# One signal per two steps: TensorE raises `summed` on every second sum, VectorE adds two banks per signal

## The reference

```python
def gnn(h, edge_index, W, b):               # h = layernorm(x)
    src, dst = edge_index
    msg_sum = segment_sum(h[src], dst, n)   # 100000 rows gathered and summed by destination
    deg = segment_sum(ones, dst, n)
    agg = msg_sum / maximum(deg, 1.0)[:, None]
    return concatenate([h, agg], axis=1) @ W.T + b

def ffn(x):                                 # x = layernorm of the first layer's result
    xn = layernorm(x) * gamma + beta
    logits = xn @ Wr + br
    w, idx = softmax of the top 2 of 8 logits
    for e in range(8):
        y += (gelu(xn @ W1[e] + b1[e]) @ W2[e] + b2[e]) * w_of(e)
    return y

x = x + gnn(layernorm(x)); x = x + ffn(layernorm(x))
```

## Time and profile before

| what | us |
|---|---|
| median of 3 runs | 1471.27 (1469.2 to 1472.08) |
| the profiled execution's own time | 1469.85 |
| its span, first to last instruction | 1468.5 |
| TensorE busy | 1154.8 (79%) |
| GpSimd busy | 1076.8 (73%) |
| VectorE busy | 766.6 (52%) |
| ScalarE busy | 501.5 (34%) |
| mean granted clock of TensorE | 0.904 |

### The profile page before, as it was taken

The page is one execution under the profiler, slowest core; times in us unless marked ns, Lnnn a source line. Parts: engine busy times, 40 slices in busy tenths (PEclk is TensorE's granted clock), DMA queues, the critical chain, the costliest instruction groups (busy, mean ns, idle before and its releaser), DMA issues.

```text
span 1468.5 us, 22976 instructions
## 1 busy us (share of the span) xinstructions
PE 1154.8 (79%) x5570; PEld 881.0 (60%) x5570; DVE 766.6 (52%) x2642; ACT 501.5 (34%) x1088; POOL 1076.8 (73%) x1032
## 2 busy tenths in 40 slices
PE   3277898779767987697979768888897978878895
PEld 2234535547535776376768547656776766656795
DVE  7666645645553555346446534644646465554321
ACT  3500004103202442144335215324353444345574
POOL 2477777677777777777777777777777777773677
PEclk9999998889877999789999869989998988988998
DMA  9943665344444554445455454545454454453444
GB/s 333 300 138 105 227 199 168 115 129 124 120 127 129 135 122 123 120 124 135 123 134 120 120 129 123 130 116 137 123 131 122 120 130 125 120 126 92 70 70 44
DMA packets 125080, 197.46 MB, mean 134 GB/s; under 512 B 23954, under 2 KB 94023, under 8 KB 124711
## 3 DMA queue, kind: packets, MB, share of 16 engines
q0 software_dynamic: 63088, 130.30, 36.4%
q1 hardware_dynamic: 59417, 64.89, 14.0%
q10 hardware_dynamic: 2446, 0.80, 0.2%
HBM read 153.82 MB, written 49.27 MB: 138 GB/s over the span
## 4 chain that ended last, share of the span: by engine, by line
PE 49%; issue 13%; POOL 13%; DVE 12%; DMA 7%; ACT 4%; DVEq 2%; ACTq 0%; POOLq 0%; SPq 0%
PE psum L736 17%; PE psum L805 11%; PE psum L830 9%; POOL work L629 7%; DMA work<-h_rows,srcs 4%; PE psum L749 4%; DVE acc L1082 3%; POOL queue L638 3%; POOL out_dram L649 2%; PE psum L750 2%; POOL out_dram L657 1%; PE psum L784 1%; ACT region L534 1%; PE psum L817 1%; PE psum L761 1%
## 5 line engine op out<-in xcount | busy, mean ns | idle before, releaser
L629 POOL DMA_INDIRECT work<-h_rows,srcs x719 | 687.9, 957 | 220.4 <-issue 178.6
L1082 DVE TENSOR_TENSOR acc<-acc,psum 128x257 f32 x830 | 349.5, 421 | 509.7 <-PE psum L736 458.4
L736 PE MATMUL psum<-work 128*128 128x257 f32 x1438 | 468.3, 443 | 140.5 <-DMA work<-h_rows,srcs 70.8
L736 PEld LDWEIGHTS psum<-work 128*128 128x128 f32 x1438 | 270.8, 212 | 256.7 <-DMA work<-h_rows,srcs 123.1
L805 PEld LDWEIGHTS psum<-expert_buf 128*128 128x128 f32 x1680 | 227.2, 212 | 12.6 <-ACT expert_buf L589 5.2
L805 PE MATMUL psum<-expert_buf 128*128 128x128 f32 x1680 | 231.1, 297 | 3.0 <-ACT expert_buf L591 1.4
L830 PE MATMUL psum<-region,expert_buf 128*128 x840 | 202.1, 384 | 3.0 <-ACT expert_buf L591 3.0
L597 ACT ACTIVATE expert_buf<-psum,b_col 128x128 f32<-128x128 f32 x420 | 120.1, 370 | 204.4 <-PE psum L805 201.7
L830 PEld LDWEIGHTS psum<-region,expert_buf 128*128 128x128 f32 x840 | 154.8, 194 | 22.0 <-issue 4.6
L971 DVE TENSOR_TENSOR work<-psum,rel 128x1152 f32<-128x1152 f32 x98 | 126.3, 1289 | 50.6 <-PE psum L736 32.1
L649 POOL DMA_INDIRECT out_dram<-expert_buf,tok_idx x75 | 121.8, 1623 | 22.9 <-issue 20.7
(11 more groups left out here) (245 smaller groups left out, 914.6 us busy)
## 6 DMA issues: line engine op xcount, KB each, us to landing
expert_buf<-queue SPq DMA_DIRECT2D x105, 130.0 KB, 2.7
work<-h_rows,srcs POOLq DMA_INDIRECT x719, 2.8
region<-in_L_ffn_W_dram SPq DMA_DIRECT2D x16, 512.0 KB, 6.4
h_rows<-region SPq DMA_DIRECT2D x7, 896.0 KB, 9.0
own<-h_rows SPq DMA_DIRECT2D x49, 128.0 KB
own<-x_rows SPq DMA_DIRECT2D x49, 128.0 KB
out_dram<-acc SPq DMA_DIRECT2D x49, 128.0 KB, 2.8
region<-in_x_dram SPq DMA_DIRECT2D x6, 896.0 KB, 11.8
```

Of the source, the lines that this page charges most:

```text
L629: pool.indirect_dma_start(place_of(g)[:, 0:D], None, h_rows, bass.IndirectOffsetOnAxis(srcs[:, cell_of:cell_of + 1], 0)).then_inc(got[g % ...
L736: summed.up(pe.matmul(STEP_BANKS[t % BANKS][:, 0:GW], hot[:, k, :], rows, start=True, stop=True))
L1082: added.up(dve.tensor_tensor(sums, sums, STEP_BANKS[t % BANKS][:, 0:GW], ALU.add))
```

## The change

Steps are taken in pairs (2m, 2m+1). Only the matmul of the odd step raises `summed`, and every wait for a step's matmul becomes a wait for its pair:

```diff
     BANKS = 3
+    TOGETHER = 2
+    assert STEPS % TOGETHER == 0
...
+    def signal_of(t):
+
+        return t // TOGETHER
...
 (sync_stream, w1 and w2)
-                    summed.wait(sp, BOTH - 1)
+                    summed.wait(sp, signal_of(BOTH - 1))
-                    summed.wait(sp, BOTH + EXTRA - 1)
+                    summed.wait(sp, signal_of(BOTH + EXTRA - 1))
...
 (gpsimd_stream)
                 if g >= SHARED + EXTRA + RING:
-                    summed.wait(pool, t - RING)
+                    summed.wait(pool, signal_of(t - RING))
...
 (tensor_stream)
                 added.wait(pe, t - BANKS)
-                summed.up(pe.matmul(STEP_BANKS[t % BANKS][:, 0:GW], hot[:, k, :], rows, start=True, stop=True))
+                i = pe.matmul(STEP_BANKS[t % BANKS][:, 0:GW], hot[:, k, :], rows, start=True, stop=True)
+                if t % TOGETHER == TOGETHER - 1:
+                    summed.up(i)
...
 (vector_stream)
                 if k == 0:
...
-                    summed.wait(dve, t - 1)
+                    summed.wait(dve, signal_of(t - 1))
                     one_hot(HALF, SPR - HALF, t + HALF)
...
-                summed.wait(dve, t)
+                summed.wait(dve, signal_of(t))
                 added.wait(dve, t - 1)
                 added.up(dve.tensor_tensor(sums, sums, STEP_BANKS[t % BANKS][:, 0:GW], ALU.add))
```

## The result

| kernel | median | runs |
|---|---|---|
| before | 1470.33 us | 4 (1469.2 to 1472.08) |
| changed | 1520.51 us | 4 (1518.01 to 1521.96) |

The ratio is 1.0342, with a 95% interval of 1.0322 to 1.0361: 50 us slower. The forecast was 1490, its range 1475 to 1508. The direction was right, the size was not, and the time is outside the range. The profiled execution took 1519.08 us (span 1517.8), 49.2 us more than the one of before.

A forecast was written before the change was run, and what follows sets the result against it. GpSimd's gathers were taken to bound 303 to 1167 us, TensorE's sums and VectorE's adds 69 to 282 us. Terms 9 + 4 + 2 + 5 + 0 = +20 us on 1469.85 us gave 1490, range 1475 to 1508.

The forecast's parts named there:

- The loop of two steps over three banks: Add, bank freed, next sum: with pairs two steps to close, 1.41 us a pair in place of 1.27.
- The first 112 steps: Pair loop 5 us, start 0.8, three odd register boundaries 3.8; taken as 9 us, bounds 4 and 12.
- Steps 112 to 219: 36 steps at 0.07 us, routing choice 0.85, some loss at long TensorE items: 4 us, between 0 and 8.
- Time lost on TensorE or VectorE in this stretch is taken out of that slack: 303 to 1167 us, GpSimd the bound: 50 to 80 us of TensorE's time against 193 us slack; 2 us taken.
- Some 85 steps: 1167 to 1331 us, 14 expert tiles, no slack toward gathers: 5 us, bounds 0 and 11.6.
- The middle: 303 to 1167 us: no GpSimd wait over 0.3 us, TensorE's gather waits down to 110 to 140; 2 us.
- Signals: TensorE raises 415 counts less: saving 0 by the trace, 11 us as an estimate from the skill page.
- The tail: After the last step, 138 us without steps: unchanged, 0 us.
- A: Loss stays in the first stretch, gathers absorb the rest: +9 to +12 us, 1479 to 1482; chance 0.22.
- B: Middle tips over, GpSimd stopped again and again: 1528 with half of 80 us unhidden, 1504 with a fifth; chance 0.13.
- C: Hidden anyway, VectorE the slower even with pairs: within 3 us, 1468 to 1474; chance 0.08.
- D: Faster by the clock, half-clock time going in 160 to 282 us and at the end: 1461; chance 0.07.

The follow-up runs named there:

- late adds: Kernel before with all signals kept, but VectorE's add of step t waits for the sum of t|1: 1.0312 and, on another chip, 1.0276.
- the two runs that divide the late adds: Kernel before, even steps' adds late only at 143 steps with other VectorE items behind the add (1.0112), or only at the other 272 (1.0172).
- coarser ring wait: Kernel before, but GpSimd waits for the sum of (t-17)|1 before gather t, where it waited for t-17: 1.001.
- bias-first: Kernel before with four banks, one-hot build from SBUF, single signals, and VectorE's bias add ahead of the step's add: 1515.11 us, 1.0287.

## Why the prediction had the direction right and the size wrong

The terms beside what the lateness table gives:

| term | forecast (bounds) | measured |
|---|---|---|
| steps 0 to 111 | +9 (4 to 12) | +12.1 |
| steps 112 to 219 | +4 (0 to 8) | +9.6 |
| 303 to 1167 us, up to step 638 | +2 (0 to 12), with the next | +1.1 |
| 303 to 1167 us, steps 639 to 745 | in the line above | +11.8 |
| steps 746 to 829 | +5 (0 to 11.6) | +10.7 |
| tail | 0 | +3.9 |
| sum | +20 | +49.2 |

*The loop of two steps over three banks* is right, and shown for the first stretch. 1.41 us a pair was forecast and read. Two banks with single signals, which have the same loop and no late add, take 82.4 us for steps 24 to 111, late adds 80.8, and with a fourth bank the pairs take 74.4, where four banks with single signals take 71.7.

*The first 112 steps* reached the top of the bound. Row by row, the three boundaries cost 1.13, 1.12 and 1.08 us (3.8 forecast for the three), the start 0.45 (0.8), and all the rest 8.3, where I had taken 5. The gather at the ring's end showed it at once, with 12.95 us.

*Steps 112 to 219* were put too low. I priced 36 steps at 0.07 us. With late adds only where neither step of a pair has an item (34 of the 54 pairs) the stretch is 4.8 us longer, about what was forecast for all; with the other 20 pairs it is 9.6. So the other half comes with pairs that have VectorE items, 12 of them right behind the late add, and I had counted one such item, the routing choice. That half is read from one profile each, and the one without it had a granted clock of 0.90 there against 0.87, so part of it can be the clock.

*The step that failed* is "Time lost on TensorE or VectorE in this stretch is taken out of that slack", with the slack read as 193 us, together with "Some 85 steps" without slack behind it. The 193 us counted each wait twice. The matmuls stood 70.4 us for gathers, and the loss that was to go into them was put at 50 to 80. Nor does slack lie in a sum from which losses are paid wherever they fall. A loss is hidden only if the sums catch up with the gathers once more after it. The last catch-up of before is at 1167 us, step 745, but all except 5.9 of the 70.4 us lie ahead of 988 us, step 639. I took the last catch-up from before's trace as fixed. With the loss it moved back to step 639 (1009 us), and the stretch in which each loss counts grew from 85 steps to 190. Its added part, steps 639 to 745, brought 11.8 us. That 36.3 us of the matmuls' waits were left, all ahead of it, shows that their sum was no measure. The move is read from the two traces; no run on a chip like this one had late adds in these steps alone. With only 20 of their 95 pairs late the sums still catch up there, last at 1181 us.

Of the 29.2 us that the forecast fell short by in the profiled execution, 10.9 are in this term (12.9 against 2, over its bound of 12), 5.7 in steps 746 to 829, 5.6 in steps 112 to 219, 3.9 in the tail and 3.1 in the first 112 steps.

*The price of a step without slack* was 0.07 us, and 0.4 us for an expert tile, of which I took less than half; 10.7 us came in steps 746 to 829, just inside the bound I had not believed. Over the 190 steps it is 22.8 us, 0.12 a step. What makes it is open. Late adds from step 640 on cost 15 us (10 to 20) by themselves on the other chips, and TensorE's waits for adds rise from 24.3 to 69.8 us. The loop of two steps is not the whole of it. Over the whole program two banks cost 31 and 33 us where late adds cost 50 and 56, and a fourth bank leaves the pairs 34. In this stretch two banks took 404 and 406 us against 406 and 407.

I had expected the rest in what stands behind a late add on VectorE. Against that stand the two runs that divide the late adds: the 46 with an item right behind them gave no rise of the waits and 407.0 us, the other 49 gave the rise and 410.6 us. Neither stretch is clear of the spread of unchanged ones, and over the whole program both kinds cost about the same for each late add (20 us for 143, 31 for 272).

On a chip like that of the result only the 20 pairs with no item at either step were run. The stretch took 338.9 us, at a granted clock of 0.92 and with TensorE busy 279.65 us against 285.56. With those 5.9 us given back, an estimate, it is +2.5. So most of the loss comes with the other 75 pairs; whether by the adds themselves, which TensorE waits for, or by items that start later, no run tells. The bias add, taken ahead of the late add, gave 5 us of 57. Open too is the part of the lower clock. The late adds from 640 have a granted clock of 0.83 beside 0.82 and are 19 us longer, with hardly more busy time (311.0 against 309.1 us), so the cost does not need the clock.

*The middle* up to step 638 was hidden, as forecast: GpSimd's waits there stay at 0.3 us, its gathers keep one lateness, and TensorE's waits for gathers halved (96 us, if loads and matmuls are added as in the forecast of 110 to 140). On the other chips, where the sums have no slack, late adds in these steps cost 25 us.

*Signals* are worth nothing here, as the rows said. The estimate by the Trainium skill's page "TensorE: Matmul & The Clock Gate", section "The cost: per-tile semaphore tail", was 11 us, 0.6%; all signals kept gave 1.0312 and 1.0276, half of them gave 1.032. By the page the last should be lower by 0.006. It is not.

*The tail* was to stay at 138 us and grew by 3.9. Its beginning did not change: GpSimd's first scatter starts 11.6 us after the last add in before and 11.7 in the changed kernel. The loss comes in its last 90 us, where GpSimd waits 15.9 us for earlier scatters into the output to land (9.7 before), at a granted clock of 0.90 (0.92). What moved them is not settled. In the runs with late adds on the other chips the tail took 138.7 and 139.1 us, against 138.4 and 139.1 without them, so the 3.9 us may be chance.

*The rivals.* A (loss stays in the first stretch) fell with step 639. B named the right danger with the wrong price and place: GpSimd was not stopped in the middle; the sums ran out of slack from behind. C and D are out: the first stretch grew by 12.1 us, and the clock was 0.904 in both. The mark I set, "if the last gather is more than 20 us later, the middle is" wrong, was met by 29.4 us, but does not say by itself where: 21.2 of them were there at step 219, and the 12.9 us of the middle show in the adds and not in the gathers up to step 745.

No version here beats the kernel before.

## What to carry to other kernels

Where a chain runs with slack behind a faster or slower partner, find the last point at which it catches up, and ask how far an added loss moves that point; only the loss ahead of the new point is hidden. Count a wait once: where a weight load and its matmul wait for the same transfer, only the matmul's wait is idle time of the engine. A signal made coarser costs a buffer's depth, and more than that: here giving the bank back saved some 20 of 50 to 57 us. The first wait for a full ring reads the loss of everything ahead of it directly.

## What the runs showed of the hardware

One-hot builds on VectorE with both operands in SBUF lengthened 60 of 782 gather issues on GpSimd, up to 2.01 us from 0.95, all gathers by 40.3 us, and with them the kernel by about 3% where GpSimd is the bound (bias-first and a fourth bank were in the same run). One operand in PSUM, as in the kernel before, avoids it.

The kernel before took about 1470 us on some chips and 1782 to 1806 on others. There, adds of the first stretch that are 0.63 us apart become 4 to 5 us apart, here in the kernel with the coarser ring wait:

```profile
74.52 0.42 DVE L1082 TENSOR_TENSOR acc<-acc,psum 128x257 f32 x1 [0.21 <-issue]
75.16 0.42 DVE L1082 TENSOR_TENSOR acc<-acc,psum 128x257 f32 x1 [0.21 <-DVE acc L1082]
79.80 0.42 DVE L1082 TENSOR_TENSOR acc<-acc,psum 128x257 f32 x1 [4.23 <-remote]
84.70 0.42 DVE L1082 TENSOR_TENSOR acc<-acc,psum 128x257 f32 x1 [4.47 <-remote]
```

Steps 0 to 23 take 102.1 us there and 19.0 here. No run tells the cause. The ratios of the changed kernel are alike on both (1.0342 and 1.032), but by different parts: the first 220 steps cost 21.7 us here and 7 (-1 to 15) there, the middle 1.1 here and 25 there, the last 190 steps 22.8 here and 15 there.
